# Two fused layers on one core: new hand-written call orders for the second layer, and two square weights loaded in quarters

## What is computed

```python
xn = layernorm(x)
x = x + L0_attn(xn) + L0_ffn(xn)
# L0_attn: static = xn @ W.T; per head (16 of width 8) a recurrence over the tokens with state S [8, 8]:
#   S = lam*S;  S += beta * k (x) (v - k^T S);  o = k^T S;   then layernorm(static + o) * w + b
# L0_ffn: h = silu(z1) * z2;  h = gelu(h @ h1.T);  h = gelu(h @ h2.T);  h @ w3.T   (hidden width 512)
xn = layernorm(x)
x = x + L1_attn(xn) + L1_ffn(xn)
# L1_attn: causal scores (q k^T) * decay(query position), times v, no softmax, 16 heads of width 8; then Wo
# L1_ffn: xn @ (W + C V_r^T).T + b
```

## Time and profile before

| | before |
|---|---|
| runs, us | 793.08, 796.32, 797.32; median 796.32 |
| the profiled execution's own time, us | 794.45 |
| its span, first to last instruction, us | 792.7 |
| busy in the span: PE, DVE, ACT, POOL | 92%, 92%, 74%, 81% |
| mean granted TensorE clock | 0.969 of full |
| bytes moved | 75.75 MB, 96 GB/s on average |

### The profile page before, as it was taken

The page is one execution under the profiler, slowest core; times in us unless marked ns, Lnnn a source line. Parts: engine busy times, 40 slices in busy tenths (PEclk is TensorE's granted clock), DMA queues, the critical chain, the costliest instruction groups (busy, mean ns, idle before and its releaser), DMA issues.

```text
span 792.7 us, 13057 instructions
## 1 busy us (share of the span) xinstructions
PE 725.8 (92%) x3325; PEld 518.4 (65%) x3325; DVE 726.5 (92%) x2036; ACT 588.9 (74%) x1363; POOL 642.8 (81%) x640
## 2 busy tenths in 40 slices
PE   3988889589999999999999999778699999999998
PEld 2544434367878888888888888653356666666555
DVE  5879897899999999999999999996788888899887
ACT  7878786679878988988988898784576466657731
POOL 3667797797888897979898899657699779889873
PEclk9989998899999999999999999996999999999999
DMA  6577865620410716143162060611623202111001
GB/s 166 184 254 241 230 209 188 163 46 14 107 56 24 146 40 146 40 100 86 40 114 67 9 142 27 168 41 24 188 75 94 67 27 81 54 59 35 1 28 41
DMA packets 136073, 75.75 MB, mean 96 GB/s; under 512 B 74826, under 2 KB 118860, under 8 KB 136012
## 3 DMA queue, kind: packets, MB, share of 16 engines
q1 hardware_dynamic: 134956, 74.58, 34.1%
q10 hardware_dynamic: 1056, 0.52, 0.2%
HBM read 39.86 MB, written 33.55 MB: 93 GB/s over the span
## 4 chain that ended last, share of the span: by engine, by line
DVE 46%; PE 26%; issue 4%; POOL 2%; ACT 2%; POOLq 0%; DVEq 0%; ACTq 0%; SPq 0%
DVE r_rec L1251 11%; DVE r_pg L1237 9%; DVE r_kw L1257 9%; DVE r_gain L1263 9%; PE f_ps L2407 7%; PE f_ps L2408 6%; DVE r_rec L1271 6%; PE f_ps L2384 4%; PE r_rec L2436 1%; PE r_rec L2442 1%; DVE l_qs L1325 1%; PE r_rec L2426 1%; PE f_ps L2415 1%; POOL l_kv L1650 1%; PE f_ps L2375 1%
## 5 line engine op out<-in xcount | busy, mean ns | idle before, releaser
L1650 POOL TENSOR_TENSOR l_kv<-l_qkv 128x1024 f32<-128x1024 f32 x64 | 124.8, 1954 | 21.5 <-PE f_ps L2408 19.5
L1251 DVE TENSOR_REDUCE r_rec<-r_pg 128x32 f32<-128x288 f32 x256 | 112.5, 440 | 0.6 <-ACT r_pg L1869 0.6
L1325 DVE TENSOR_TENSOR l_qs<-f_ps,l_qd 128x1024 f32<-128x1024 f32 x64 | 78.2, 1221 | 27.5 <-PE f_ps L2408 20.8
L1263 DVE TENSOR_REDUCE r_gain<-r_kw 128x64 f32<-128x256 f32 x256 | 101.9, 398 | 0.0
L2271 PE MATMUL f_ps<-f_gh,w_hi 128*128 128x512 f32 x256 | 100.0, 391 | 1.4 <-POOL f_gl L1522 1.3
L1522 POOL TENSOR_TENSOR f_hl<-f_h,f_hh 128x512 fp32r<-128x512 f32 x64 | 81.1, 1304 | 23.7 <-ACT f_hh L1915 23.4
L2271 PE MATMUL f_ps<-f_hh,w_hi 128*128 128x512 f32 x256 | 99.9, 390 | 0.0
L1530 POOL TENSOR_TENSOR f_g<-f_a,f_b 128x512 f32<-128x512 f32 x64 | 82.5, 1300 | 16.9 <-ACT f_b L1904 16.7
L1522 POOL TENSOR_TENSOR f_gl<-f_g,f_gh 128x512 fp32r<-128x512 f32 x64 | 82.8, 1308 | 0.0
L1332 DVE TENSOR_REDUCE l_o_in<-l_qs 128x128 f32<-128x1024 f32 x64 | 77.2, 1211 | 0.5
L2407 PE MATMUL f_ps<-l_kv,tri 128*128 128x512 f32 x128 | 67.8, 612 | 8.3 <-POOL l_kv L1650 5.1
(11 more groups left out here) (227 smaller groups left out, 2104.0 us busy)
## 6 DMA issues: line engine op xcount, KB each, us to landing
scratch_xnT<-p_xnT SPq DMA_DIRECT2D x16, 256.0 KB, 2.3
scratch_K<-p_kout SPq DMA_DIRECT2D x16, 256.0 KB, 2.4
scratch_fac<-p_fac SPq DMA_DIRECT2D x16, 256.0 KB, 2.0
scratch_R<-p_rr SPq DMA_DIRECT2D x16, 256.0 KB, 3.0
scratch_P<-p_pp SPq DMA_DIRECT2D x16, 256.0 KB, 2.3
first_x<-scratch_xnT SPq DMA_DIRECT2D x16, 256.0 KB, 3.6
first_xt<-in_L_attn_x_dram SPq DMA_DIRECT2D x16, 256.0 KB, 3.0
scratch_W<-r_w SPq DMA_DIRECT2D x16, 256.0 KB, 4.3
```

Of the source, the lines that this page charges most:

```text
L1251: dve.tensor_reduce(w_here(g, blk), pg[q][:, at, :, :, :].rearrange("p (v g) i k -> p v g i k", g=G)[:, :, g, :, :], AX.X, ALU.add).then_i ...
L1263: dve.tensor_reduce(of_group(g, gain), of_group(g, kw), AX.X, ALU.add).then_inc(gain_ok, 1)
L1325: dve.tensor_tensor(qs[s % 2][:, :].rearrange("p (h v k) -> p h v k", h=H, k=DH), score_banks(s)[:, :, :].rearrange("p a (h v k) -> p (a h ...
L1650: pool.tensor_tensor(dst, k, v, ALU.mult).then_inc(kv_ok, 1)
```

## The change

It does three things. In the preparation each square weight comes in four DMAs of 256 KB (128 columns of all 512 rows, in pieces of 512 bytes), one in each of the steps 1 to 8, each three steps ahead of the transposes that use it; w3 comes in step 9. In the second layer the lists of DVE, POOL, ACT and PE are written anew from the end of the feed-forward part on and the loops in their middles are gone. Each list holds the same calls, with the same arguments, as before (the loops counted out). SP's list stays. `residual(0)` waits in addition for POOL's own last `hidden_rest`.

```diff
         mats = [(nat12[:, 0, :, :], io["L0_ffn_w1_w"].rearrange("(o p) i -> p o i", p=P)),
...
+        for w, name in enumerate(("L0_ffn_h1_w", "L0_ffn_h2_w")):
+            rows = io[name].rearrange("(o p) i -> p o i", p=P)
+            mats += [(nath[:, w, :, i * P:(i + 1) * P], rows[:, :, i * P:(i + 1) * P]) for i in range(NB)]
+        mats += [(nat3[:, :], io["L0_ffn_w3_w"])]
...
-        MATS_AT = {1: 2, 4: 3, 7: 4}
+        MATS_AT = {g - 1: g for g in range(2, NG)}
...
+        def arrived(g):
+
+            if g < 2:
+                return mat_in[g], 16
+            if g == NG - 1:
+                return mat_in[4], 16
+            return mat_in[2 + g % 2], 16 * (g // 2)
...
+                def load_weights(g):
+                    if 2 + 2 <= g < NG - 1:
+                        sp.wait_ge(*arrived(g - 2))
+                    sp.dma_start(*mats[g]).then_inc(arrived(g)[0], 16)
...
                     if k in MATS_AT:
-                        sp.dma_start(*mats[MATS_AT[k]]).then_inc(mat_in[MATS_AT[k]], 16)
+                        load_weights(MATS_AT[k])
...
                 def weights(g):
-                    pe.wait_ge(mat_in[of_mat[g]], 16)
+                    pe.wait_ge(*arrived(g))
...
         def residual(u):
             pool.wait_ge(yw_ok, u + 1)
+            if u == 0:
+                pool.wait_ge(hl_ok, last.count(NB, NB))
```

More of the change, by code:

```diff
@@ L2495, in tensor @@
         second(last, 1)
+        biased()
         second(last, 2)
+        outputs(2)
         second(last, 3)
         normed(0)
[L2499 removed]
+        output(last)
         project(0, 0)
[L2501 removed]
         project(0, 1)
[L2503 to L2504 removed]
+        normed(1)
         project(0, 2)
[L2506 to L2507 removed]
         project(1, 0)
```

986 lines of the change are left out of this document (593 added, 393 removed).

## The result

| | before | after |
|---|---|---|
| runs in this comparison | 20 | 20 |
| median, us | 794.29 | 800.07 |
| lowest and highest, us | 791.06, 797.32 | 795.56, 803.91 |
| span of the profiled execution, us | 792.7 | 796.0 |

The ratio is 1.0061, with a 95% interval from 1.0045 to 1.0076: 4.9 us lost on 794.3. The forecast was 789.4 in a range of 782.5 to 798.0, so both its sign and its range were wrong. The two profiled executions stand 3.3 us apart.

The account below looks back on a forecast made before the run. It took a 7.7 us loop step to bound the preparation, DVE the recurrence, and PE (20.00 of 20 us) the second layer. -2.1 - 3.3 - 1.5 = -6.9 us from 796.3 gave 789.4, range 782.5 to 798.

Parts of the forecast that it names:

- Preparation, -2.1: Weight loading before the recurrence: 3.0 us won in steps 5 and 6, 0.9 lost to added quarters; bounds -3.0 and +1.
- place (b): Recurrence's end: `save_w(30)` behind `total2(2)` ends at 547.7, the recurrence 2.3 us later, hidden in part by PE's `busy`.
- The transition, -3.3: Recurrence's end to `running(0,3)`: 4.0 us gained by better packing, less 0.7 for the lower clock; bounds -6 and +3.
- (a): Transition: `output(15)` ends at 534.4, `project(0,0)` follows ten us later than before, at no cost by itself.
- (c): Transition: `root_table` before `save_w(31)`; `outputs(3)` near 555.6, `running(1,1)` 562.3, `running(1,2)` 568.6, `running(0,3)` 571.9, a gain of 4.0 us.
- the third rival: Transition gives nothing: after a PE hole the lower clock stretches `output(15)` to up to 7.5 us; 792.8 us, chance 0.20.
- half a chance of 1.4: Transition: PE's lower clock, a loss of 1.4 us in the old order, may recur in the new; counted as 0.7.
- The steady part, -1.5: Second layer after the transition: fewer PE stalls between two `running`, 1.5 us won; bounds -5 and +11.
- a quarter of the best case: Steady part: of the old 6.5 us of stalls nearly all could go at best; a quarter taken, -1.5 us.
- the fourth rival: Steady part: small DVE products held by POOL's `outer` make DVE the bound, 11 us over 12 blocks; 802 us, chance 0.13.
- The sign to look for: Profile after: mean durations of L1298 and L1316 (`scale1`, `scale2` products) above 1.2 would show the forecast wrong.

Follow-up runs that it names:

- pointer: Changed kernel with each small product of `scale1` and `scale2` done as four one-column products by a per-partition scalar; 0.9979 of the kernel before.
- quarters: Kernel before with only the square weights loaded in quarters, old lists kept; 0.9969 of the kernel before.
- after_filled: Changed kernel with unread matmuls in three PE holes of the transition (two, three and two); 1.0029 of the kernel before.
- save_first: Changed kernel with `save_w(30)` moved in front of `norm1(2)` on ACT; 1.0071 of the kernel before.
- after_filled_five: Changed kernel with unread matmuls in three PE holes of the transition and five small products done column by column; 0.9999 of the kernel before.
- five_pointer: Changed kernel with only five of 28 small products done column by column (`scale1` of 8, 16; `scale2` of 3, 9, 10); 1.0002 of the kernel before.
- quarters_pointer: Kernel before, old lists, with weights in quarters and all small products done column by column by a per-partition scalar; 0.9962 of the kernel before.
- four_filled_b: Kernel before with weights in quarters, four small products column by column, unread matmuls before `running(0,0)` (four) and `normed(1)` (one); 0.9894 of the kernel before.

## Why the prediction was wrong

**Preparation, -2.1: right in its sum, not in its working.** The recurrence started 2.0 earlier. The block loads of steps 5 to 8 stand at 42.69, 51.07, 59.04 and 67.87 in the changed kernel, 8.38, 7.97 and 8.83 apart, where step 6 took 9.76 before. At the load of step 7 the changed kernel was 3.7 ahead. Steps 7 to 10 then took 36.0 us, where they took 32.5 before, and gave 3.5 of it back; I had put down 0.9 for the added quarters. At the last block load (110.33 against 110.52) 0.2 was left. The other 1.8 arose behind it, where the change loads nothing: from the last load to the recurrence it took 38.8 instead of 40.6. That stretch took 38.5 to 38.8 us in eight of the 15 profiles with quarters and 40.8 to 41.3 in the other seven, though the preparation is the same program in all of them. In the long ones the clock was lower for longer: from 112 to 126 us the granted clock was 0.88 in the changed kernel and 0.76 in `pointer`. So it was luck that the two profiles gave 2.0 by this sum. That the quarters gain is shown by the timing of `quarters` (0.9969, 0.8 to 4.2 us); by which way is open.

**The wait for `save_w(30)`, place (b): right in time by luck, and free.** `save_w(30)` was to end at 547.7 and ended at 547.54. The stall is 4.16 and not 2.3, because the recurrence came 2.0 earlier. I had reckoned all times of the transition without the preparation's gain and then added that gain at the end. The 2.0 were made up for by the slower `output(15)`, which stands ahead on ACT's chain: in `after_filled`, where it ran at full clock, the wait was 1.69. That it did no harm is shown by `save_first`: the wait was hidden.

**The transition, -3.3: measured +0.4. The steps that failed are (a), "It costs nothing by itself", and in (c) "`running(1,2)` near 568.6".** `output(15)` was put down at full clock, 3.73, after a stretch in which I had myself counted only 0.5 us of PE work. It took 6.10 at a granted clock of 0.50, as the third rival said, and `project(0,0)` followed at 534.19, where 532.3 (534.4 less the 2.1) was due. Then the chain to unit 3: `outputs(3)` on PE, forecast for 555.6, came at 555.33, without the 2 us of the preparation. `running(1,1)` came at 562.48, where 562.3 less the 2.0 was due: 2.2 late, and `after_filled` wins just these 2.2 up to there. That is one pair of profiles; `after_filled_five` wins only 0.6 over `five_pointer` up to the same point, so the size of this step is less sure than its direction.

The rest of the miss lies between `running(1,1)` and `running(1,2)`: 8.45 us, where (c) had 6.3. PE waited 3.08 for `norm2(3)`, behind a product of `scale2(3)` that took 1.41 beside an `outer`, and then worked at the lower clock. In `after_filled` the interval is 7.3, with the wait and without the lower clock; in `five_pointer`, where that product is split, it is 6.4, with a wait of 2.12 and full clock. So 1.1 are the clock, for which the sum had half a chance of 1.4, and 0.9 the held product, which I had priced in the steady part alone.

**The steady part, -1.5: measured +4.8. The step that failed is the choice between the terms, "I take a quarter of the best case".** I had counted the fill between two `running` with care, and it did not decide: with the small products out of `outer`'s way the same new list has 7.0 us of stalls instead of 11.3. But the fills did not win either. The old list with the same repair has 4.3, so the new one is behind by 2.7 even so; what holds it there is open. The greater part of the loss is the fourth rival's mechanism at about half its price: 5.7 us of stalls in four places (0.88 + 1.18 + 1.80 + 1.84), instead of 11 spread over 12 blocks. Each costs up to a whole `outer` of 1.95, less the step's slack (an estimate from these rows). I had dismissed it with "only 26 such instructions, and most stand behind `scores`"; four that do not are enough. By the rule of the Trainium skill's page "SBUF — State Buffer", section "SBUF: two separate sides", the one of the two instructions that comes second is blocked until the other is done. The trace agrees: the products end with the `outer` (657.23 and 657.21).

**The sign to look for was wrong too.** I had named mean durations above 1.2 for these two lines. They stayed at 0.65, because a mean over 13 says nothing of which four met an `outer` in front of a `scores`.

**The rivals.** The result is the third and the fourth at once: the third's lower clock with nothing won in the transition, and the fourth's held products. They have different places and nothing makes them exclude each other, yet I gave each a chance as if only one could come (0.20 and 0.13), and let the range end where one of them alone would. Together with the 2.0 of the preparation, and with the measured sizes, they are the +3.4 above.

**What the new order is worth by itself.** With the products repaired, `pointer` (new lists) and `quarters_pointer` (old lists) are 0.9979 and 0.9962; with both repairs, `after_filled_five` and `four_filled_b` are 0.9999 and 0.9894. The first pair is even within its intervals, the last is 8 us apart; in neither is the new order ahead. The repairs are not the same in the last pair: five products and seven unread matmuls there, four and five here. Of the 9.1 us between the spans of the last pair, 6.6 are stalls (10.3 against 3.7) and 2.1 the transition (1.0 later, with 1.1 of work still to do). Whether a longer choice of products would bring the new lists level was not tried.

## What to carry to other kernels

Before an order is changed for its packing, list the instructions whose duration depends on what runs beside them, and check in the new order which of them stand in front of the engine that bounds; a mean over the group will not show them. Price work moved across a hole at both levels of the clock, since the same hole can be followed by either. A stage that ends earlier in one profile is not yet shown to be faster: time it. A long wait on an engine is a loss only if the next engine was ready: undo it alone before it is blamed.

## What was not expected of the hardware

- A product of one column by a per-partition scalar in SBUF was never held up by POOL's `outer`: 110 of them took 202 to 215 ns, where the form with two tensor inputs took 0.16 to 2.00 us. Four cost 0.58 us in place of 0.16.
- Matmuls that nobody reads, four (3.60 us) and one (1.10 us), made the old transition 3.4 us shorter (426.0 to 422.6) in one profile each. In the new order two, three and two of them made it 3.3 shorter in one pair and 1.1 longer in the other.
- The spread between executions of one kernel goes with the granted clock. Of the 131 timed ones of the kernel before that stand beside the experiments, the 17 with a mean granted clock below 0.962 took 798.0 us on average, the 56 with 0.971 or more 793.0.
- The start of the recurrence differs by kernel though the preparation is the same program: 147.1 to 152.2 us over the 15 kernels with quarters (mean 149.1), 151.1, 151.2 and 152.7 with whole weights. A single profile could not have told the 2 us of the quarters; the timed rounds did.
